# Prologue clears, two gate weights staged in the accumulator, and two more pieces in the chain of a perceiver kernel

## The reference

```
x = x + xattn0(layernorm(x), ctx)        # 64 queries against 1601 keys, per batch; 16 heads
x = x + attn0(layernorm(x))              # small attention among the latents
x = x + ffn0(layernorm(x))               # top-1 of 8 experts, relu
x = x + xattn1(layernorm(x), ctx)        # as xattn0, with biases
x = x + ssm1(layernorm(x))               # s_t = s_(t-1) A^T + B u_t; gelu, layernorm, nan_to_num
x = x + moe1(layernorm(x))               # gate, up and down: each a top-2 of 8 experts

# moe1: g = sum_e c_g[:, e] * (x @ w_gate[e].T); u = the same with w_up
#       inter = silu(g) * u; d = sum_e c_d[:, e] * (inter @ w_down[e].T)
```

## Time and profile before

| | us |
|---|---|
| three runs | 975.91, 975.71, 983.85 (median 975.91) |
| the profiled execution | 971.84 |
| its span | 969.8 |
| the profiled execution outside its span | 2.04 |
| PE busy in the span | 905.1 (93%) |
| DVE, ACT, POOL busy | 636.2, 521.0, 144.4 |

### The profile page before, as it was taken

How to read it: one execution, slowest core, us unless ns; L and a number is a source line. 1 busy time by engine, 2 the same in 40 slices (tenths; PEclk the granted TensorE clock), 3 DMA queues, 4 the chain that set the end, 5 groups by cost and what they waited for, 6 DMA issues and landing times.

```text
span 969.8 us, 34389 instructions
## 1 busy us (share of the span) xinstructions
PE 905.1 (93%) x14880; PEld 576.6 (59%) x14880; DVE 636.2 (66%) x1103; ACT 521.0 (54%) x986; POOL 144.4 (15%) x177
## 2 busy tenths in 40 slices
PE   5699899989999999999999999998898999998998
PEld 2366565656665665666666566666443444447887
DVE  5676665766676466758667776777569677776622
ACT  5387767677676676666657756745542432212300
POOL 5311212121111111121212211310000000000000
PEclk9999999999999999999999999999899999999999
DMA  8877486454634544544345344425223233221200
GB/s 310 234 251 240 106 262 180 108 163 113 183 93 149 130 95 125 130 103 126 84 133 142 100 119 109 133 58 184 78 99 130 68 109 128 88 87 52 81 1 22
DMA packets 70839, 123.76 MB, mean 128 GB/s; under 512 B 34770, under 2 KB 46082, under 8 KB 67428
## 3 DMA queue, kind: packets, MB, share of 16 engines
q1 hardware_dynamic: 69524, 119.22, 41.5%
q0 software_dynamic: 592, 1.42, 0.4%
q10 hardware_dynamic: 576, 0.94, 0.4%
HBM read 64.88 MB, written 17.32 MB: 85 GB/s over the span
## 4 chain that ended last, share of the span: by engine, by line
PE 74%; DVE 12%; ACT 6%; issue 5%; DMA 1%; SPq 1%; ACTq 1%; POOL 0%; DVEq 0%
PE ps L755 72%; DVE mpart L1365 3%; ACT p L1115 3%; ACT ch L1082 1%; DMA c32b<-in_ctxT 1%; DVE cl L1344 1%; DVE acc L1413 1%; SPq L524 1%; ACT kh L1099 1%; ACT k L1098 1%; DVE v L1356 1%; PE ps L901 1%; DVE w16a L1396 1%; DVE x L1465 0%; ACTq L1262 0%
## 5 line engine op out<-in xcount | busy, mean ns | idle before, releaser
L1365 DVE TENSOR_REDUCE mpart<-ps 128x2 f32<-128x800 f32 (+1 forms) x256 | 252.8, 989 | 124.7 <-PE ps L755 122.7
L1115 ACT ACTIVATE p<-ps 128x512 f32<-128x512 f32 (+1 forms) x416 | 225.8, 596 | 180.9 <-PE ps L755 177.7
L704 POOL TENSOR_TENSOR kl<-k,kh 128x400 f16<-128x400 f32 (+1 forms) x128 | 118.3, 925 | 375.2 <-ACT kh L1099 375.2
L755 PE MATMUL ps<-p,v 128*17 128x64 f32 x6656 | 131.2, 221 | 0.0
L755 PE MATMUL ps<-wvh,ch 128*128 128x256 f16 (+1 forms) x416 | 115.0, 277 | 5.2 <-issue 5.2
L755 PEld LDWEIGHTS ps<-p,v 128*17 128x17 f32 x6656 | 97.7, 98 | 37.4 <-issue 36.6
L755 PE MATMUL ps<-wvl,ch 128*128 128x256 f16 (+1 forms) x416 | 114.0, 274 | 0.4 <-issue 0.4
L755 PE MATMUL ps<-wvh,cl 128*128 128x256 f16 (+1 forms) x416 | 114.0, 274 | 0.0
L755 PEld LDWEIGHTS ps<-qcur,ks 64*128 64x128 f16 (+1 forms) x3328 | 61.4, 97 | 67.2 <-issue 51.7
L755 PE MATMUL ps<-w16a,xmh 128*128 128x512 f16 x320 | 96.4, 383 | 3.5 <-DVE w16a L1396 3.5
L755 PE MATMUL ps<-kh,qbcur 64*128 64x400 f16 (+1 forms) x512 | 86.4, 335 | 13.6 <-DVE mpart L1365 10.4
(11 more groups left out here) (211 smaller groups left out, 1329.6 us busy)
## 6 DMA issues: line engine op xcount, KB each, us to landing
ks<-kh SPq DMA_DIRECT2D x252, 100.1 KB
w<-in_wgu SPq DMA_DIRECT2D x16, 1024.0 KB, 4.9
ks<-kl SPq DMA_DIRECT2D x126, 100.1 KB
w<-in_wd SPq DMA_DIRECT2D x8, 1024.0 KB, 4.9
c32a<-in_ctxT SPq DMA_DIRECT2D x16, 400.5 KB, 5.0
cparts<-ch SPq DMA_DIRECT2D x8, 800.5 KB, 6.9
cparts<-cl SPq DMA_DIRECT2D x8, 800.5 KB, 8.7
c32a<-in_ctxT SPq DMA_DIRECT2D x12, 400.0 KB, 3.4
```

The source lines that it names most:

```text
L704: nc.gpsimd.tensor_tensor(kl[:, mt, k0:k0 + w], k32[:, ku % 2, 0:w], kh[:, mt, k0:k0 + w], ALU.subtract).then_inc(sem("klo_done"), 1)
L755: return nc.tensor.matmul(o, lhsT, rhs, start=start, stop=stop, skip_group_check=shared)
L1115: nc.scalar.activation(p32[0:n, step % PRING, BANK * side:BANK * side + BANK], ps[0:n, side, :], ACT.Exp, scale=DH ** -0.5).then_inc(sem(" ...
L1365: nc.vector.reduce_max(mpart[:, j0:j0 + 3:2, quarter], o.rearrange("p (b c) -> p b c", b=2)[:, :, 0:w], AX.X).then_inc(sem("max_done"), 1)
```

## The change

**At the front.** The clears of `fb` and `ones16` go to DVE's first instructions. PE waits for `pv_clear` ahead of the first W and no longer ahead of V2. P11 goes ahead of N0, P12 ahead of N1, P14 to P13, P15 ahead of N3, and N3 behind T. ACT splits context pieces 6 and 7 one unit earlier. Of the 12 DMAs of round 0's second restack SP issues 9 and ACT 3.

**At the end of the loop.** The first two weights are loaded at step (12, 0) into a dead part of `acc` (which holds no sums yet), weight 2 alone at (15, 1). Weight 0 is split at step (14, 10), weight 1 at (15, 7). Pieces start at step (15, 6): seven in the loop where six were.

**In the chain and the tail.** `m_stats` is followed by two pieces and `m_norm` by one, where it was one and none. The split of weight 18 leaves the final turns and goes 11 pieces before the last list's end.

```diff
-PROLOGUE_UNITS = ("Q K0 K1 P0 K2 P1 K3 P2 K4 P3 K5 P4 K6 P5 K7 P6 V0 P7 P8 V1 P9 P10 N0 P11 N1 P12 P13 N2 P14 N3 "
-                  "P15 T").split()
-FIRST_CTX_HIGH = {"K4": 4, "K6": 5, "V0": 6, "V1": 7}
+PROLOGUE_UNITS = ("Q K0 K1 P0 K2 P1 K3 P2 K4 P3 K5 P4 K6 P5 K7 P6 V0 P7 P8 V1 P9 P10 P11 N0 P12 N1 P13 P14 N2 P15 "
+                  "T N3").split()
+FIRST_CTX_HIGH = {"K4": 4, "K6": 5, "K7": 6, "V0": 7}
...
-SPLIT_AT = {(G - 1, 6): 0, (G - 1, 9): 1}
-PIECES_AT = {(G - 1, k): k - 7 for k in range(7, KT)}
+SPLIT_AT = {(G - 2, 10): 0, (G - 1, 7): 1}
+PIECES_AT = {(G - 1, k): k - 6 for k in range(6, KT)}
...
+W_IN_ACC = 2
...
-         ("s_5", 1), ("s_y", 2), ("g_stats", 1), ("g_norm", 1), ("g_parts", 1), ("g_clean", 1), ("m_stats", 1),
-         ("m_norm", 0), ("m_turn", 1), ("r_logits", 2), ("r_pick", 0)]
+         ("s_5", 1), ("s_y", 2), ("g_stats", 1), ("g_norm", 1), ("g_parts", 1), ("g_clean", 1), ("m_stats", 2),
+         ("m_norm", 1), ("m_turn", 1), ("r_logits", 2), ("r_pick", 0)]
...
+    if q == len(PIECES) - 2 * TT - 3:
+        TAIL += [("h", 18), ("l", 18)]
...
-    if j >= 3:
-        TAIL.append(("turn", j - 3))
-    if j >= 3:
-        TAIL.append(("low", j - 3))
-    if j == 3:
-        TAIL += [("h", 18), ("l", 18)]
+        TAIL += [("turn", j - 3), ("low", j - 3)]
...
+        def staged(w):
+            if w < W_IN_ACC:
+                return acc[:, 1, TT - 2 * w - 2:TT - 2 * w, :].rearrange("p t c -> p (t c)")
+            return w32[:, w % 3, :]
...
-            restack(0, 1, range(2))
+            restack(0, 1, range(3))
...
+                    if (g, k) == (G - 4, 0):
+                        sp.wait_ge(sem("clo_done"), 4 * B)
+                        sp.wait_ge(sem("f_mm"), 4 * TT)
+                        for w in range(W_IN_ACC):
+                            load(staged(w), weight(w), f"w_in{w}")
                     if (g, k) == (G - 1, 1):
                         sp.wait_ge(sem("main_mm"), 2 * KT * (G - 1))
-                        for w in range(3):
-                            load(w32[:, w, :], weight(w), f"w_in{w}")
+                        load(w32[:, 2, :], weight(2), "w_in2")
...
+                if g == 0 and k == 0:
+                    pe.wait_ge(sem("pv_clear"), 1)
+                    pe.wait_ge(sem("v_ones"), 1)
...
-            pe.wait_ge(sem("pv_clear"), 1)
...
                 if w == 0:
+                    act.wait_ge(sem("v_mm"), V_UNITS * (G - 1))
+                elif w == 1:
...
-                    for j in range(2, 4):
+                    for j in range(3, 4):
...
+            nc.vector.memset(fb[64:97, :], 0.0).then_inc(sem("fb_clear"), 1)
+            nc.vector.memset(ones16[64:97, :], 1.0).then_inc(sem("ones16"), 1)
             dve.wait_ge(sem("x_in"), 16)
...
-            nc.vector.memset(fb[64:97, :], 0.0).then_inc(sem("fb_clear"), 1)
-            nc.vector.memset(ones16[64:97, :], 1.0).then_inc(sem("ones16"), 1)
-            dve.wait_ge(sem("v_ones"), 1)
             dve.wait_ge(sem("max_done"), 2 * NP)
             nc.vector.memset(pvb, 0.0).then_inc(sem("pv_clear"), 1)
```

More of the change, by code:

```diff
@@ L1131, in split_w @@
                     act.wait_ge(sem("part_mm"), last + 1)
-                nc.scalar.activation(w16(w, 0), w32[:, w % 3, :], ACT.Copy, scale=W_SCALE)\
+                nc.scalar.activation(w16(w, 0), staged(w), ACT.Copy, scale=W_SCALE)\
                    .then_inc(sem("whi_done"), 1)
@@ L1138, in part_first @@
                 act.wait_ge(sem("cmb_done"), PIECES[q][1] + 1)
+                act.wait_ge(sem("wlo_done"), W_IN_ACC)
                 nc.scalar.activation(part_acc(q), ps[:, part_bank(q), :], ACT.Copy, scale=part_coefficient(q))\
@@ L1395, in split_w @@
                 dve.wait_ge(sem("whi_done"), w + 1)
-                nc.vector.scalar_tensor_tensor(w16(w, 1), w32[:, w % 3, :], W_SCALE, w16(w, 0),
+                nc.vector.scalar_tensor_tensor(w16(w, 1), staged(w), W_SCALE, w16(w, 0),
                                                ALU.mult, ALU.subtract).then_inc(sem("wlo_done"), 1)
@@ L1589, in event @@
                     nc.vector.nop().then_inc(sem("cmb_done"), 1)
-                elif name == "part" and t:
+                elif name == "part" and t and not first_by_act(t - 1):
                     part_add(t - 1)
             nc.vector.memset(m16[:, :], 0.0)
+            nc.vector.memset(fb[64:97, :], 0.0).then_inc(sem("fb_clear"), 1)
+            nc.vector.memset(ones16[64:97, :], 1.0).then_inc(sem("ones16"), 1)
             dve.wait_ge(sem("x_in"), 16)
```

## The result

The changed kernel takes 971.4 us (median of 15 runs) beside 976.61 us for the kernel before (15 runs): a ratio of 0.9938, with a 95% interval of 0.992 to 0.9957. By the ratio that is 6.1 us off (0.0062 x 976.61), by the profiled executions 4.3 (971.84 to 967.57; the spans went from 969.8 to 965.3). Forecast were 7.0 us off, and a time of 968.9 in 963 to 976. One of the 15 runs after took 2181.18 us, for no reason that is on record; the ratio leaves it out, and the median without it is 970.7.

What follows compares the result with a forecast made beforehand. PE, working in 93% of the span, was taken as the bound, leaving only its idle places to gain. Front -0.7, loop end -1.6, chain -2.5 and turns -2.2 gave 7.0 us off 975.9: 968.9, range 963 to 976.

Steps and rivals of the forecast that it cites:

- Front: Part A: 2.0 us kept of 5.3 gained, less 1.3 for the clock: -0.7, between -5.3 and +0.5.
- what is late next is data: Front: context piece 10, last load of SP's burst, lands at 65.6 and holds up ACT's split, leaving 2.0 of 5.3 us.
- costed at nothing and at most at 1.0: Front: P11 ahead of N0 makes PE wait longer for DVE's maxima; taken as free, at most 1.0 us.
- The clock term (1.3): Front: PE's clock falls after new idle time of about 3.5 us at 66 to 69.5; costs 1.3, between 0 and 2.0.
- End of the loop: Part B, weight 0 split earlier: -3.0 by sum, -2.85 taken, with 1.3 for the clock -1.6, between -2.9 and +0.5.
- 2.8 for the wait and 1.3 for the clock: Round 14's end: DVE's low half delays P14, P15, T, so S(15, 0) comes 2.8 us later; lower clock costs 1.3.
- The rival on the clock: PE falls to 1.2 GHz at both new idle places, 2.0 us each; chain's pieces only move the wait; 973, chance 0.22.
- doesn't do what it says: Rival: weight 0's wait moves from round 15 to round 14's row chain; B +0.5, 971.0; inside forecast's range, no own chance.
- Chain: Part C, last tile: two more pieces fill waits of 3.9 us in all, less 1.4 for DVE's adds: -2.5, between -3.9 and 0.
- Turns: Part C, final turns: weight 18's split taken out removes PE's 2.26 us wait for the second turn: -2.2, between -2.5 and 0.
- The burst rival: Front: the burst moves at 203 GB/s instead of 310, piece 10 lands at 78; +5.4 in all, 981, chance 0.06.
- the first rival: Front keeps its 5.3 us because piece 10 is not late; sum -11.6, 964.3, chance 0.22.

Runs made afterwards that it cites:

- run 9: Kernel before with the front alone changed (order of units, clears, wait for `pv_clear`, restack); ratio 0.9982.
- run 1: Changed kernel with the stores of batch 0's split context issued right behind round 0's restack; ratio 0.9891.
- 3: Changed kernel with the restack of round 0's second half divided 6 and 6 between SP and ACT again; ratio 0.9941.
- run 5: Kernel before with the end of the loop alone changed, weight 0 split at (14, 10); ratio 0.9998.
- Run 4: Changed kernel with the low half of weight 6 moved from behind the last tile's routing to three pieces later; ratio 0.9894.
- run 8: Changed kernel, batch 0 stores first, weight 0 split at (14, 12), weight 6's low half later, restack 6 and 6, batch 1 stores behind piece 10; 958.87 us.
- run 6: Kernel before with the chain and the turns alone changed (two more pieces, weight 18's split out of the turns); ratio 0.9972.
- run 10: Kernel before with the end of the loop alone changed, but weight 0 split at (14, 12); ratio 0.9952.
- run 11: Kernel of run 8 with two weights' loads moved from round 2, step 0 to round 1, step 10; 960.38 us, ratio 0.9835.

## Why the prediction was right, and where its sizes were off

The range and the direction held. By the two profiles the parts give 4.5 us where 7.0 were forecast; the turns came out as reckoned, the other three parts too small, for the reasons below. The timed runs, at 6.1 us, lie nearer to the forecast, and that is partly luck: the profile from which the sum was worked out had a faster front than the three others with the same front (last section).

- **Front** (forecast -0.7; measured -0.43 between the two profiles; -2.1 at the P unit between the means of four profiles with the old front and four with the changed one; -1.8 by the timed runs of 9, whose interval takes in 0). The step "what is late next is data" held, and so did its numbers: piece 10 landed at 65.1 (issued 56.72, 8.4 us) where 65.6 was forecast. But it was not what ACT waited for. The step named the last DMA of the burst; an earlier one, the store of batch 0, holds back a buffer that ACT writes at step (0, 3), four steps ahead of the split of piece 10. Runs 1 and 3 show it. S(0, 0) came at 42.01, 1.0 late: P15 stood at 38.79, no earlier than before, since PE reached P13 and P14 at 37.22 only. What held it up is the wait of 3.31 us for P11 and the half clock behind it, which the prediction had costed at nothing and at most at 1.0: it was the 1.0, so T ended at 41.79, as before, and not at 40.9. The clock term (1.3) was about right for the place it was meant for, (0.31 + 0.12) x 4 us is 1.7; that the clock would fall in the prologue as well was not in the sum.
- **End of the loop** (forecast -1.6; measured -0.8, which is 2.1 less the chain's 1.34, and 0 alone in run 5). That the low half blocks the row chain was right to half a microsecond: DVE was to be free at 667.1 and was at 666.6 with the front 0.43 ahead. S(15, 0) came 4.3 us later (3.86 + 0.43), where 2.8 for the wait and 1.3 for the clock were taken, 4.1 in all; but it is made up otherwise. The new idle time is 2.0 us more than before, not 2.8. The term that was mis-sized is the clock: from S(14, 12) to S(15, 0) the same work of PE took 5.15 us instead of 2.85, so 2.3 and not 1.3. S(15, 0) did not wait for T in the end, which was through at 670.51: V2 of round 15 stands ahead of it and took 2.65 us at half clock (1.3 at full clock before). The rest is on the side of the gain, 5.1 us instead of 5.7, as PE waits a little longer for exponentials in round 15. The rival on the clock had the price; the rival "doesn't do what it says" had the place. The Trainium skill's rule ("TensorE: Matmul & The Clock Gate", "What's actually happening": the throttled clock is the default) speaks for that price, and this trace agrees: PEclk 0.64 and 0.51 behind the new idle time.
- **Chain** (forecast -2.5, measured -1.34). The first wait closed as said. The second was to shrink, and grew from 1.62 to 2.27: the adds of the pieces that PE has done ahead stand behind routing and a split of 2.29 us on DVE, and more pieces ahead mean more adds there. Run 4 takes that split away and the wait with it. I had put the two waits in one sum, although a different instruction of DVE ends each. Besides, two more pieces are only 2.6 us of PE's work, so of the 3.9 no more than that could be filled. Less the 1.4 for DVE's adds that is 1.2 by the prediction's own figures, near the 1.34 measured.
- **Turns** (forecast -2.2, measured -2.0). As worked out.

The burst rival fell: stores and piece 10 landed within 3 us of their old times. That piece 10 is in time (the first rival) needs the move of run 1 and more. In run 8, where ACT does not wait for it, the P unit starts at 66.99, 4.6 us ahead of the profile of before, of the 5.3 that this rival had; at S(14, 0) 3.8 are left.

## What to carry to other kernels

When a wait at the front goes, list every buffer that the next engines write and read in the following 30 us, with what frees each, and not only the last transfer of the burst: the one that decides is the first to be late. Put a split or another long instruction behind the row that others wait for, even if that is two steps later: the split of weight 0 cost 4.4 us more in step 10 than in step 12. And where two waits lie behind one another, ask for each which instruction ends it before adding them up.

## What the runs showed of the hardware that I had not expected

**The profile of before was a lucky one.** Its time was 971.84 us, the median of its runs 976.61. Runs 5, 6 and 10 have the old front too, and their P unit behind piece 10's split starts at 74.19, 74.84 and 75.34, not 71.63. All three have a wait of PE that the profile of before lacks, within the multiplications with `wq` (timeline of PE, 48 to 78 us, of runs 5, 6 and 10):

```profile
56.82 0.94 PE L764 MATMUL ps<-xnT,wq 128*128 128x128 f32 x6 [1.78 <-issue]
```

```profile
57.06 1.57 PE L755 MATMUL ps<-xnT,wq 128*128 128x128 f32 x6 [2.05 <-issue]
```

```profile
56.72 1.65 PE L764 MATMUL ps<-xnT,wq 128*128 128x128 f32 x6 [2.53 <-issue]
```

No instruction, semaphore or transfer of the kernel ends it. The DMA engines are full there, and in the listing of DMA by queue the packet of the instruction queue q8 ahead of this place (16 KB; its row gives packets, MB and share of 16 engines) lies in 54 to 55 us in run 6, and in 52 to 53 us in the profile of before, which has no wait:

```profile
q8 instruction: 1, 0.02, 6.8%
```

```profile
q8 instruction: 1, 0.02, 7.0%
```

The same is seen once more at one instruction of round 2, where the wait is 2.95 us in run 1 (PE goes on at 131.28; the packet is in 128 to 129 us), 2.12 in run 9, 1.85 in run 8, 0.76 in the profile of before, and none in that of after. So PE may be waiting for its own program, which would come through the same engines as the data. That is argued from the times that go together; run 11, which was to show it, did not, and the cause stays open. What is shown is that a front with the engines full is one place where two executions of one kernel differ by 3 us (run 10 is 9.2 us behind the profile of before at S(14, 0), of which 3.7 stand at the P unit already), and that one profile says little on a gain of that size.

**The clock falls at idle times of different length.** It fell after waits of 2.25 us at the front and 2.89 us (in two parts) at 664 to 668, and not in run 1 after 1.46 us at 67.93. The length of the wait alone does not settle it. Ahead of S(14, 0) PE stands for 1.5 us in the same order of work in all 13 profiles; behind it the clock fell in five (runs 5, 6, 9, 10 and 11) and not in the other eight. The window of 634 to 636 us, before and in run 9, with S(14, 0) at 632.02 and 632.33 behind 1.51 us of waiting in both:

```profile
634.00:636.00 2.00, 2.00 (x60) 1.47 (x57) 1.73 (x10) 0.73 (x3) 0.00 (x0) 1.00 0.66 159
```

```profile
634.00:636.00 2.00, 2.00 (x13) 1.39 (x10) 1.02 (x9) 0.21 (x1) 0.00 (x0) 0.54 0.60 155
```

What tells these executions apart stays open.
